# GpSimd makes the A operands of the top-k distances a tile ahead, and the next batch's normalised rows

## The reference, cut to what matters

```
x = x + attn_a(layernorm(x))      # 16 heads of width 8, full softmax over 1024 keys
x = x + ffn(layernorm(x))         # weights of +1/-1: 256 -> 512 -> 512 -> 128
x = x + attn_b(layernorm(x))      # 8 heads of width 16, the 32 nearest of the last 64 tokens
x = x + ffn(layernorm(x))
```

```
kw = q_h[:, idx, :]                                   # the last 64 tokens of each token
wsq = (kw - q_h[:, :, None, :]) ** 2 * metric
dist = sqrt(wsq.sum(-1) + 1e-08)
neg, loc = top_k(-dist, 32)
infl = exp(-topd); infl = infl / infl.sum(-1)
context = sum over k of infl * v_h[topi]
```

## Time and profile before

| what | value |
|---|---|
| median of 3 runs | 2972.43 us (2961.26, 2972.43, 2973.3) |
| the profiled execution | 2964.93 us, its span 2963.2 us |
| mean granted TensorE clock in it | 0.921 |
| busy share: PE, ACT, DVE, POOL | 81%, 76%, 71%, 23% |
| one turn in the middle | about 348 us, of which the second half about 145 us |

### The profile page before, as it was taken

The page is one execution under the profiler, slowest core; times in us unless marked ns, Lnnn a source line. Parts: engine busy times, 40 slices in busy tenths (PEclk is TensorE's granted clock), DMA queues, the critical chain, the costliest instruction groups (busy, mean ns, idle before and its releaser), DMA issues.

```text
span 2963.2 us, 60847 instructions
## 1 busy us (share of the span) xinstructions
PE 2411.7 (81%) x21171; PEld 1048.0 (35%) x21171; DVE 2112.0 (71%) x10282; ACT 2263.2 (76%) x3151; POOL 688.7 (23%) x869
## 2 busy tenths in 40 slices
PE   4788778888788887988888897888888888887666
PEld 1112242244332443334432443324433344224444
DVE  5801778957797668966789577876689667982695
ACT  4798668977699677987689776996779877994432
POOL 3020115111251114401152112511134011311331
PEclk6599789999899999999889998999999999999887
DMA  3011001100011001210011000110012000000000
GB/s 87 30 46 43 2 19 48 50 18 6 23 56 43 17 8 28 65 31 9 20 44 54 18 6 23 54 42 17 6 35 65 31 9 12 14 17 1 17 20 11
DMA packets 98518, 84.79 MB, mean 29 GB/s; under 512 B 19954, under 2 KB 79540, under 8 KB 98212
## 3 DMA queue, kind: packets, MB, share of 16 engines
q1 hardware_dynamic: 97968, 80.41, 9.2%
q10 hardware_dynamic: 244, 0.49, 0.1%
HBM read 55.32 MB, written 25.44 MB: 27 GB/s over the span
## 4 chain that ended last, share of the span: by engine, by line
ACT 34%; PE 33%; DVE 19%; issue 6%; POOL 5%; SPq 2%; DMA 0%; ACTq 0%; DVEq 0%; POOLq 0%
PE banks L802 30%; ACT PT L1141 17%; DVE xn L1473 4%; ACT pq L1128 4%; DVE h L1476 3%; DVE pq L1260 2%; ACT xn L1086 2%; ACT hparts L1152 2%; POOL Aop L781 2%; PE banks L809 2%; ACT h L1153 2%; ACT h L1054 1%; DVE h L1458 1%; ACT Bs L1054 1%; POOL qkf L728 1%
## 5 line engine op out<-in xcount | busy, mean ns | idle before, releaser
L1141 ACT ACTIVATE PT<-banks 128x1024 f32<-128x1024 f32 x1024 | 996.6, 1038 | 47.4 <-PE banks L802 44.7
L1260 DVE CUSTOM_DVE_ANT_0 pq<-pq,banks 128x512 f32<-128x512 f32 x1024 | 653.4, 683 | 175.5 <-ACT pq L1128 174.8
L1128 ACT ACTIVATE pq<-banks 128x1024 f32<-128x1024 f32 x512 | 523.2, 1023 | 223.5 <-PE banks L802 198.1
L802 PE MATMUL banks<-PT,Vg 128*9 128x512 f32 x4096 | 545.9, 605 | 2.3 <-ACT PT L1141 2.3
L802 PE MATMUL banks<-Q,K 51*128 51x512 bf16 x2048 | 391.0, 393 | 139.9 <-ACT PT L1141 113.3
L802 PE MATMUL banks<-K,Q 48*128 48x512 bf16 x2048 | 360.9, 431 | 80.6 <-ACT pq L1128 37.2
L762 POOL TENSOR_TENSOR hparts<-h,hparts 128x512 fp32r<-128x512 f32 x112 | 140.5, 1272 | 1009.2 <-ACT h L1153 1009.2
L1473 DVE MATCH_REPLACE8 xn<-h,xn 128x96 f32<-128x96 f32 x1536 | 352.2, 241 | 0.0
L802 PE MATMUL banks<-hparts,W 128*128 128x512 f32 x1024 | 303.9, 426 | 39.6 <-ACT h L1153 27.8
L802 PEld LDWEIGHTS banks<-Q,K 51*128 51x128 bf16 x2048 | 96.2, 93 | 620.4 <-ACT PT L1141 534.9
L1476 DVE MAX8 h<-xn 128x8 f32<-128x96 f32 x1536 | 263.0, 243 | 0.0
(11 more groups left out here) (207 smaller groups left out, 3256.3 us busy)
## 6 DMA issues: line engine op xcount, KB each, us to landing
Vw<-scratch_v SPq DMA_DIRECT2D x256, 51.0 KB, 2.1
scratch_k<-pq SPq DMA_DIRECT2D x24, 384.0 KB, 3.1
K<-scratch_k SPq DMA_DIRECT2D x126, 72.0 KB
qkf<-in_hidden_states SPq DMA_DIRECT2D x16, 512.0 KB, 4.4
scratch_q<-pq SPq DMA_DIRECT2D x24, 256.0 KB, 2.3
Q<-scratch_q SPq DMA_DIRECT2D x126, 48.0 KB
K<-scratch_k SPq DMA_DIRECT2D x126, 48.0 KB
scratch_v<-Bs SPq DMA_DIRECT2D x8, 544.0 KB, 3.5
```

Of the source, the lines that this page charges most:

```text
L802: return pe.matmul(o, l, r, start=start, stop=stop)
L1128: act.activation(cut(g), ring_pair if work is TURN0 and g % 2 else pair[0], ACT.Relu).then_inc(diff_out.sem, 1)
L1141: act.activation(PT[:, at:at + 2, :], pair[g % ESLOTS], ACT.Exp, scale=1.0 if i % 8 < 4 else -1.0).then_inc(probs.sem, 1)
L1260: dve.tensor_tensor_reduce(r, r, pair[1 + g % 2][:, par, :], 1.0, -3.0e38, ALU.subtract, ALU.max, mred[:, par, i, qt:qt + 1]).then_inc(max ...
```

## The change

Three things are changed.

1. **`lnn` of side h goes from ScalarE to GpSimd**, for batches 1 to 7 (batch 0 is made in `FIRST` and stays). GpSimd waits for the same factors and issues eight `tensor_scalar` (multiply, add).
2. **The places of `aop`, `dist` and `dev` in `SLOTS_T`.** `dist` of tile u+1 goes from the second slot of tile u to the third, `dev` from the third to the fourth, and `aop` of tile u+2 stands in the fifth slot of tile u. Of tile 1, `aop` goes one slot later. In `SLOTS_P`, `aop` of tile 0 goes ahead of `keys`.
3. **A few weights of `WEIGHTS["P"]`** (entries 60 to 74) are other numbers, and their sum is 0.57 larger. In the first half of each turn this swaps some `max` stages with a neighbour of side p.

The turns 2 to 6 are now numbered one by one; that changes no instruction.

```diff
 SLOTS_T = []
 for _u in range(NU + 1):
-    _next, _last, _here = _u + 1 < NU, _u >= 1, _u < NU
+    _start, _next, _last, _here = _u == 0, _u + 1 < NU, _u >= 1, _u < NU
...
-        (3.0, [(_u >= 2, "decd", _u - 2), (_next, "aop", _u + 1), (_here, "vload", _u), (_here, "top", (_u, 0))]),
-        (2.0, [(_next, "dist", _u + 1), (_here, "top", (_u, 1))]),
-        (2.5, [(_next, "dev", _u + 1), (_here, "top", (_u, 2))]),
-        (2.5, [(_last, "wt", _u - 1), (_here, "top", (_u, 3))]),
-        (2.0, [(_last, "pv", _u - 1), (_here, "top", (_u, 4))]),
+        (3.0, [(_u >= 2, "decd", _u - 2), (_here, "vload", _u), (_here, "top", (_u, 0))]),
+        (2.0, [(_start, "aop", 1), (_here, "top", (_u, 1))]),
+        (2.5, [(_next, "dist", _u + 1), (_here, "top", (_u, 2))]),
+        (2.5, [(_next, "dev", _u + 1), (_last, "wt", _u - 1), (_here, "top", (_u, 3))]),
+        (2.0, [(_u + 2 < NU, "aop", _u + 2), (_last, "pv", _u - 1), (_here, "top", (_u, 4))]),
...
+                    if (side, stage) == ("h", "lnn") and work is not FIRST:
+                        pool.wait_ge(*coef_a.at(b, 1))
+                        for u in range(NU):
+                            ins = pool.tensor_scalar(xna[:, u, :], xa[:, u, :], ls[:, 0, 6, u:u + 1], ls[:, 0, 7, u:u + 1],
+                                                     ALU.mult, ALU.add)
+                        ins.then_inc(xn_a.sem, 1)
...
-                    if stage == "lnn":
+                    if stage == "lnn" and (side != "h" or work is FIRST):
```

More of the change, by code:

```diff
@@ L230 @@
 FIRST, FIRST_USE, _k = numbered(HEAD, 0)
-TURN0, TURN0_USE, _k0 = numbered(phases(True, False, False), _k)
-NR = sum(uses(stage, n) for _, stage, n in phases(True, True, True))
-TURN1, TURN1_USE, _k1 = numbered(phases(True, True, False), _k0 - NR)
-TURN, TURN_USE, _ = numbered(phases(True, True, True), _k1 - NR)
-TURN7, TURN7_USE, _k7 = numbered(phases(False, True, True), _k1 - NR)
-LAST, LAST_USE, _ = numbered(TAIL, _k7)
-assert NR % 2 == 0
+TURN0, TURN0_USE, _k = numbered(phases(True, False, False), _k)
+TURN1, TURN1_USE, _k = numbered(phases(True, True, False), _k)
+TURNS = []
+for _c in range(2, NB - 1):
+    _work, _use, _k = numbered(phases(True, True, True), _k)
+    TURNS.append((_work, _use))
+TURN7, TURN7_USE, _k = numbered(phases(False, True, True), _k)
+LAST, LAST_USE, _ = numbered(TAIL, _k)
 class Count:
@@ L254, with __init__ @@
 class Ring:
-    def __init__(self, banks, sem, name, uses):
+    def __init__(self, banks, sem, name):
         self.banks = banks
-        self.ready = Count(sem(f"{name}_ready"), uses)
-        self.evicted = [Count(sem(f"{name}_evicted{i}"), uses // 2) for i in range(2)]
+        self.ready = Count(sem(f"{name}_ready"), 0)
+        self.evicted = [Count(sem(f"{name}_evicted{i}"), 0) for i in range(2)]
     def bank(self, k):
@@ L305, in hybrid_block_kernel @@
         ring_pair = banks[:, 6:8, :]
-        R = Ring(psum[6:8], sem, "ring", NR)
+        R = Ring(psum[6:8], sem, "ring")
         scratch_q = nc.dram_tensor("scratch_q", [PARTS, P, T], BF16, kind="Internal").ap()
@@ L671, in _ @@
             for c in range(2, NB - 1):
-                go(TURN, TURN_USE, c, h=c + 1, a=c, o=c - 1, p=c - 1, q=c - 2)
+                go(*TURNS[c - 2], c, h=c + 1, a=c, o=c - 1, p=c - 1, q=c - 2)
             go(TURN7, TURN7_USE, NB - 1, a=NB - 1, o=NB - 2, p=NB - 2, q=NB - 3)
```

15 lines of the change are left out of this document (8 added, 7 removed).

## The result

The changed kernel is slower. Its median is 2999.41 us (2990.98 to 3006.55, 5 runs) beside 2967.35 us of the kernel before on the same chip; the ratio is 1.0099, with a 95% interval of 1.0082 to 1.0116. The profiled execution took 2993.98 us, its span is 2992.2 us, 29.0 us more than the span before.

The account below looks back on a forecast made before the run. No single engine was taken to carry the span, with ScalarE and VectorE nearly full in steady second halves. Terms -3.0 - 6.0 - 0.8 + 4.2 - 1.5 = -7.1 us, from 2972.4, gave 2965.3 us; 8-in-10 range 2940 to 2982.

Parts of the forecast that it names:

- Part 6: First halves, turns 1 to 7: a max behind the FFN's last products delays the rows; +0.6 us a turn, +4.2 us.
- Part 4: Tile 3, turns 1 to 6: distances later in TensorE's order shrink ScalarE's gap; -1.0 us a turn, -6.0 us.
- Part 5: Steady tiles: distances and their eviction about 1.4 us later still end in time, 0.6 us left; 0.
- Part 7: Tail: the earlier A operand removes VectorE's 1.13 us wait at tile 7; -1.5 us, bounds -5 and +3.
- Part 1: Turn 0: rows on GpSimd take work off ScalarE, the limit there; -3.0 us, once.
- Part 2: Turns 1 to 6: rows on GpSimd bring TensorE's transposes 0.35 us later; +0.4 us a turn.
- Part 3: Start of second halves, turns 1 to 7: work fills part of ScalarE's 3.95 us gap; kept in turn 7, -0.8 us once.
- the rows pay in full: Turns 1 to 6: ScalarE's 3.2 us really go, 19 to 34 us faster; chance 0.15, half of it 0.10.
- GpSimd's queue becomes the bound: Tile 2's mask add and tile 3's A operand come late through slow rows; 40 us slower, 3005 us; chance 0.12.
- The shared way: Turns 1 to 6: new GpSimd rows slow a VectorE operation through shared SBUF access; 12 us at most, 2977; chance 0.05.
- Nothing moves at all: Gains at turn 0 and tile 3 are taken by the first halves; 2972 us; chance 0.13.

Follow-up runs that it names:

- f2: The kernel before with side h's normalised rows made by GpSimd in turn 0 alone; 2969.0 us beside 2967.6, ratio 1.0006.
- e4: The changed kernel with side h's normalised rows made by ScalarE again in all turns; 3003.9 us, ratio to the kernel before 1.0122.
- h1: The changed kernel with tile 2's A operand made behind the new rows in turns 1 to 7 and the tail; 2987.9 us, ratio to before 1.0052.
- f3: The kernel before with side h's normalised rows on GpSimd in turns 0 to 6, nothing else; 2964.0 us beside 2967.6, ratio 0.9978.
- g3: The kernel before with the new places of aop, dist and dev in turns 1 to 7 alone; 2969.8 us beside 2971.7, ratio 0.9992.
- f4: The kernel before with turn 0's rows on GpSimd and A operands of tiles 2 to 7 a tile early in turns 1 to 7; 2950.5 us, ratio 0.9941.
- e3: The changed kernel with the old places of aop, dist and dev in turns 1 to 7; 2998.4 us, ratio to the kernel before 1.0103.
- e1: The changed kernel with max (1,1,6) put back ahead of FFN products (0,1,0) in turns 1 to 7; 2985.8 us, ratio to the kernel before 1.006.
- f1: The kernel before with FFN products (0,1,0) put ahead of max (1,1,6) in turns 1 to 7; 2977.1 us beside 2967.6, ratio 1.0035.
- e2: The changed kernel with the old places of aop, dist and dev in the tail; 2991.5 us, ratio to the kernel before 1.008.
- g2: The kernel before with the changed kernel's tail order alone; 2978.5 us beside 2971.7, ratio 1.0032.
- g4: As g1, with the early A operands in the tail too; 2946.6 us beside 2971.7 for the kernel before, ratio 0.9927.
- g1: The kernel before with rows of turns 0 to 6 on GpSimd and A operands of tiles 3 to 7 a tile early in turns 1 to 7; 2943.8 us, ratio 0.9923.
- h3: The changed kernel with the max/FFN swap undone, old tail places, and rows on GpSimd in turn 0 only; 2968.5 us, ratio to the kernel before 0.9998.

## Why the prediction was wrong, point by point

Predicted were 2965.3 us, between 2940 and 2982; measured 2999.4. Six of the seven terms came out slower than I put them. By the profiles the sum was wrong by 36.2 us (-7.1 predicted, +29.1 found): 16.0 in the second halves of turns 1 to 6, 12.6 in the tail, 4.5 in the second half of turn 7, 2.8 in the first halves and 0.3 in turn 0. The first halves look nearly right by luck: the swap's 12 us stand in them beside turn starts that were 6.3 us shorter by the draw of the clock. The steps that failed are the swap put at nothing (part 6), a gain of the new places that `dist` and `dev` a slot later take away (parts 4 and 5), and the sign of the tail (part 7).

- **Part 1, turn 0 (-3.0): right.** -2.7 in the profile, -3.8 in f2.
- **Part 2, rows in turns 1 to 6 (+0.4 a turn): the mechanism was right, the size was not.** In turn 4, which I read, the key difference comes 0.46 us later. But 38.46 us behind the first mask add was the latest of before's turns 2 to 6; the others have 37.0 (three times) and 37.6. The changed kernel has 38.9 in all of them, so the mean cost is 1.5 us. I took one turn for six. TensorE's wait for the rows grew by 1.0 us in turn 4. My rival "the rows pay in full" had its condition right, the A operand of tile 2 not ahead of them: with it ahead the rows cost 0.8 us a turn (changed kernel against e4), with it behind they bring 0.8 (h1 against e4, which also differ in the place of that A operand) to 1.3 (f3 against before). It had the size wrong (3.2 us a turn), since TensorE still waits 2.03 us for them in h1.
- **Part 3, start of the second half (-0.8, once): too high.** ScalarE's 3.95 us became two pieces, as said, but of 0.59 and 3.23 us, 3.8 in sum, where I said about 3. In turn 7 the first eviction of `oT` comes 27.27 us behind the mask add for 27.28 before: nothing was won.
- **Part 4, tile 3 (-1.0 a turn): the step failed.** I saw that the mask add cancels the early A operand, and ScalarE's gap went. In turn 4 the residual's bias add on GpSimd comes 0.85 us earlier behind the first mask add, which looks like the term. But turn 4 of before was again a late one: over turns 1 to 6 that add comes 0.6 us later on average (113.9 us behind the first mask add for 113.3). With the rows left out, g3 has nothing of the gain either, while f4, which leaves `dist` and `dev` alone, has 2.9 us a turn.
- **Part 5, steady tiles (0): the step failed.** I let TensorE's distances move by 1.4 us and VectorE by as much. In fact they moved behind one more wait of TensorE for an Exp (1.26 us), and VectorE stands 0.72 us for them. This costs 3.7 us in turn 7 (g3 has it again, e3 is free of it); in each other turn the wait comes once, with about 0.7 us.
- **Part 6, first halves (+0.6 a turn): the step that failed most.** I priced the swap at the end of the FFN and wrote that "the other swaps exchange equal neighbours". They are equal in work, not in what they wait for: `max` (1,1,6) covered the eviction that the FFN's products want. 12 us in the profile, some 14 by e1, 9.5 by f1. Whether the 0.6 us that I did price came, no run shows.
- **Part 7, the tail (-1.5, bounds -5 and +3): wrong in sign, and outside its bounds.** +11.1 us in the profiles; the order costs some 10 (e2, g2). I read only the one wait at tile 7. VectorE is nearly full there, and loses 2.9 us to operations that stand longer beside GpSimd. That the rest comes from `dev` a slot later, with MAX steps ahead of every mask add, is argued and not shown; g4, with early A operands alone, already has 3.4 us of it against g1.
- **The rivals.** "GpSimd's queue becomes the bound" gave 3005 us, near what was measured, but did not happen as described: a row takes 0.43 us where that rival needed 0.9 and more, the distances of tile 3 don't wait, and VectorE waits for GpSimd no longer than before (1.9 us, once). "The shared way" is real, but in the tail; beside the new rows VectorE does MAX and MATCH_REPLACE steps, at their usual length. "Nothing moves at all" is the time of h3, not of the change.

## What to carry to other kernels

Two neighbours in an order are equal only if they wait for the same thing; before a swap is priced at nothing, look up which wait each of them covers, and what TensorE's clock does behind a stand. A step is only ahead if all that feeds it, and all that shares its queue, stays where it was: here early A operands with `dist` and `dev` left alone, and turn 0's rows, bring 17 us; all three moved together bring nothing. And read several repeats of a loop before one is multiplied: the one that I chose had the latest split of the five alike.

## What the runs showed of the hardware

- **A stand of under a microsecond can cost more than itself.** Behind 0.95 and 0.82 us of standing the granted clock falls in five of the six turns 2 to 7 (0.66 over 5 us in turn 4), each time for 1.5 us more; in turn 2, with the same order and the same waits, it stays at 1.00, and in h1, with the swap too, it stays there in turns 3 and 4 (39.6 us). Which of the two comes is not settled by the order of the instructions. The same holds for two other places, with 1.5 us (turn start) and 3.5 to 5 us at stake (between `sq<-qh` and the first mask add: in turn 3 of the changed kernel 34.93 us with a clock of 0.54 in the first row below, in turn 4 31.41 us with the second). I take these draws to be why executions of one kernel differ by 15 to 20 us; that no run shows directly.

```profile
1113.00:1118.00 5.00, 5.00 (x16) 2.33 (x14) 2.11 (x9) 2.55 (x5) 0.00 (x0) 0.54 0.42 82
1464.00:1469.00 5.00, 5.00 (x17) 1.58 (x16) 3.90 (x17) 4.12 (x9) 0.42 (x1) 1.00 0.45 86
```

- **VectorE and GpSimd block each other, and who starts first wins.** One 128x768 operation of VectorE with two SBUF inputs, at tile 6 of the tail: GpSimd and VectorE in the changed kernel, then the two before.

```profile
2916.21 2.50 POOL L770 TENSOR_TENSOR hparts<-Q,hparts 128x512 fp32r<-128x512 f32 x2
```
```profile
2916.48 3.04 DVE L1488 SCALAR_TENSOR_TENSOR h<-xn,h 128x768 f32<-128x768 f32 x1
```
```profile
2890.31 4.27 POOL L781 TENSOR_SCALAR Aop<-qd,alpha,minus 128x128 f32<-128x128 f32 x8
```
```profile
2890.29 0.96 DVE L1480 SCALAR_TENSOR_TENSOR h<-xn,h 128x768 f32<-128x768 f32 x1
```

After, GpSimd starts 0.27 us ahead, and VectorE's operation ends 0.81 us behind GpSimd's pair, about its own 0.96 us. Before, VectorE starts just ahead, keeps its 0.96 us, and GpSimd's eight rows take 4.27 us instead of 3.48. g2, with the new tail, has 3.04 us at the same place again, and both have one of 1.80 us: 2.9 us of the tail's 11.8. The Trainium skill, "SBUF — State Buffer", section "SBUF: two separate sides", says that the pair of ports which the two engines share is held by whichever of such operations starts first, and that the other waits. These rows agree. That section speaks of one instruction; here VectorE waited for both of GpSimd's pair. The other long A operands look alike. Before has eight of 4.1 to 4.3 us, the other 56 take 3.5 to 3.6; in each of the eight only the first row is long (1.15 to 1.26 us for 0.46), and it starts while this operation of VectorE is still there. So do the twelve of the changed kernel. The operation ahead of the A operand of the earlier trace rows, beside GpSimd's `xT<-xT,pq`, was itself held up:

```profile
1525.33 1.55 DVE L1480 SCALAR_TENSOR_TENSOR h<-xn,h 128x768 f32<-128x768 f32 x1
```

- **GpSimd makes these rows at ScalarE's pace**: eight 128x128 rows with two factors in 3.45 us, ScalarE's in 3.18.
